# A fused attention and feed-forward layer: weight loads in halves, small pieces of side work, and last-stage buffers moved

## The chip, the cores and the metric

The kernel runs on one NeuronCore of a Trainium2 chip. The metric is device time in microseconds (us) of one execution. PE is TensorE, DVE is VectorE, ACT is ScalarE, POOL is GpSimd, and SP is the engine whose queue issues every DMA of this kernel.

## The reference

The input x has 4 batches of 512 rows and 1024 columns. Everything is float32. Attention has 32 heads of 32 columns, one shared key and value head, a linear bias and a causal mask. The second part is a linear layer whose weight comes from 6-bit codes.

```
def attn(h, Wq, Wkv, Wo):
    q = (h @ Wq).reshape(b, s, 32, 32)
    k, v = (h @ Wkv)[..., :32], (h @ Wkv)[..., 32:]
    scores = einsum('bqhd,bkd->bhqk', q, k) * 32 ** -0.5 + slopes * (pos_k - pos_q)
    attn = softmax(where(pos_k <= pos_q, scores, -inf))
    return einsum('bhqk,bkd->bqhd', attn, v).reshape(b, s, 1024) @ Wo

def ffn(x, qweight, scale, zero, bias):
    w = (unpack(qweight) - zero) * scale          # 1024 x 1024 codes of 6 bits
    return x @ w.T + bias

x = x + attn(layernorm(x), Wq, Wkv, Wo)
x = x + ffn(layernorm(x), qweight, scale, zero, bias)
```

## The kernel before

Each engine has a program written out by hand; an engine waits on semaphores, and what stands behind a waiting instruction waits too. Float32 factors are split into a high and a low part (`woh` and `wol`, `osh` and `osl`, `yth` and `ytl`), and products of the parts are summed.

There are three stages. The **first** normalises x, projects it, writes q to the tensors `qh_d` and `ql_d` in DRAM, and turns the codes into a weight `wi_d` in DRAM. The **second** is attention in 32 steps; step s is group s % 8 (four heads) of batch s // 8. The **third** goes over 16 tiles of 128 rows: `out_proj(t)` multiplies by Wo, `norm(t)` adds x and normalises, `turn_y(t)` transposes, `ffn(t)` multiplies by the codes `wi`, `result(t)` adds scale, shift and bias, and `store(t)` writes.

**A step of attention.** On PE a step has 12 places: places 0 to 4 and 6 to 11 hold a unit of transposed scores (`score_t`, L586), place 5 holds `turn_max(s+1)` (L576), the transpose of the maxima of the next step. Between them lie the 16 products of `score` (L559), 28 products ahead, and the products with the values (L597) and with ones (L610, `totals`) of step s-1. The maxima of the scores come from DVE (`maximum`, L920), 16 in a step; product n may start only when DVE has taken what was in its bank of PSUM, about one head earlier. After the tenth maximum (i = 9) DVE makes `ml`, the low part of the maxima of step s+1 (`max_low`, L927); the unit at place 8 on PE waits for `ml`, since it reuses that bank. SP then sends `mh` and `ml` (L302) into rows of q of step s+1, and place 0 of that step waits for them to land. q of step s lies in `qst[s % 4]`, a quarter of `xt0`; SP loads it three steps ahead (L294, 0.77 MB in three DMAs). ACT takes the exponentials (L761, `exponentials(s, k)`, k from 0 to 10), POOL cuts them by the mask (L415) and adds them up (L422, L428).

**Side work in the steps.** SP loads two chunks of `wi` (L333, 512 KB each) in each of the steps 1 to 4. In eight steps (WO_STEPS) Wo is split: SP loads a chunk of 512 KB into `ob`, ACT rounds it (`wo_high`, L777, after k = 9) and DVE subtracts (`wo_low`, L937, 128x1024, behind the sixteen maxima). In steps 10 to 13, 18 to 21 and 26 to 29 DVE inverts a quarter of the sums of a batch (`invert`, L933). In step 26 SP issues `load_o(0)`, `load_o(1)` (L351, 512 KB each) and `load_inv(0)` (L360, four DMAs of 128 KB).

**From the second stage to the third.** PE mixes out_proj(0) into the last step and behind it, then the totals of step 31, then `out_proj(1)`. ACT ends the steps with exponentials(31, 10), then take_o, take_sums, `o_high(1)` (L799). `o_high(1)` needs `o_normal(1)` on DVE (L955), and that needs load_inv(1). SP, behind the steps: load_inv(1), store_o(31), a wait for the totals of step 31, then x for tile 0 (`load_x2`, L344), three broadcast rows (L390), x for tile 1, load_o(2), load_inv(2). All buffers of the third stage but `osh0`, `osl0`, `ob` and `inv_b` lie where `pt`, the exponentials, lay. On ACT the order is std_y(0), o_high(2), t_high(0), so ffn(0) waits for load_inv(2) by way of `o_normal(2)` on POOL (L434).

## Time and profile before

| | us |
|---|---|
| median of 3 runs | 929.73 |
| lowest and highest | 925.4, 939.7 |
| profiled execution, whole | 931.09 |
| its span, first to last instruction | 929.3 |

The profiled execution is one of its own; 1.8 us of it lie outside the span. Rows below are read against it.

### The profile page before, as it was taken

How to read it: one execution, taken by the hardware profiler on the slowest of the kernel's cores; microseconds unless marked ns; L12 is line 12 of the kernel's file. 1: busy time of each engine (PE TensorE's matmuls, PEld its weight loads, DVE VectorE, ACT ScalarE, POOL GpSimd, SP SyncE). 2: the span in 40 equal slices, each digit the busy share in tenths (PEclk: the TensorE clock that was granted, in tenths of full speed). 3: DMA queues.
4: the chain of work that ended last, by engine and by line, in shares of the span. 5: the costliest groups of instructions: out<-in, count | busy, mean ns of one | idle time of the engine just before them, and what ended most of it. 6: DMA issues, size and time to landing. Idle time of an engine off the chain costs nothing.

```text
span 929.3 us, 13775 instructions
## 1 busy us (share of the span) xinstructions
PE 872.2 (94%) x4912; PEld 628.3 (68%) x4912; DVE 542.0 (58%) x1469; ACT 335.4 (36%) x639; POOL 397.0 (43%) x254
## 2 busy tenths in 40 slices
PE   2799999999999999999999979969999999999996
PEld 2578888888855555555555545548888888888884
DVE  6454362532566787888788757126656455554553
ACT  2422222221066666667666636321211112211110
POOL 0000000000048778888888858626345433454211
PEclk9899999999979999999999979988999999999997
DMA  4544554648348754464454461175333553334111
GB/s 153 164 156 122 176 153 153 176 120 212 101 107 225 201 140 106 115 165 117 111 145 130 114 143 46 48 202 139 90 91 93 145 124 105 90 91 135 47 46 45
DMA packets 86892, 117.17 MB, mean 126 GB/s; under 512 B 8020, under 2 KB 50004, under 8 KB 86744
## 3 DMA queue, kind: packets, MB, share of 16 engines
q1 hardware_dynamic: 86824, 116.30, 46.2%
q8 instruction: 39, 0.64, 0.3%
...
## 4 chain that ended last, share of the span: by engine, by line
PE 87%; DMA 5%; DVE 5%; ACT 1%; SPq 1%; issue 1%; POOL 0%; DVEq 0%; POOLq 0%; ACTq 0%
PE p_o L505 19%; PE p_st L668 14%; PE p_st L586 10%; PE p_s L654 10%; PE p_s L559 9%; PE p_o L597 9%; PE p_o L654 8%; PE p_o L610 4%; DMA xt<-ml 2%; PE p_st L505 2%; PE p_s L498 1%; DMA raw<-in_wq_dram 1%; DVE spill L920 1%; DMA inv_b<-inv_d 1%; PE p_st L576 1%
## 5 line engine op out<-in xcount | busy, mean ns | idle before, releaser
L920 DVE CUSTOM_DVE_ANT_0 spill<-p_s,mask 128x128 bf16<-128x128 f32 (+3 forms) x512 | 225.4, 486 | 82.3 <-PE p_s L559 80.6
L415 POOL TENSOR_SCALAR_AFFINE_SELECT pt<-pt 128x512 f32<-128x512 f32 x128 | 90.1, 716 | 317.2 <-ACT pt L761 317.2
L761 ACT ACTIVATE pt<-p_st 128x512 f32<-128x512 f32 (+1 forms) x352 | 181.4, 561 | 102.0 <-PE p_st L586 96.6
L505 PE MATMUL p_o<-xt,wqh 128*128 128x512 f32 x512 | 171.8, 402 | 3.7 <-DVE wql L1021 3.7
L559 PE MATMUL p_s<-kst,xt 98*128 98x128 f32 (+3 forms) x512 | 152.3, 336 | 6.5 <-DVE mx L920 6.5
L586 PE MATMUL p_st<-xt,kst 100*128 100x512 f32 (+1 forms) x352 | 148.5, 425 | 8.4 <-DMA xt<-ml 6.4
L505 PEld LDWEIGHTS p_o<-xt,wqh 128*128 128x128 f32 x512 | 98.3, 192 | 24.8 <-DVE wql L1021 4.1
L559 PEld LDWEIGHTS p_s<-kst,xt 98*128 98x128 f32 x512 | 101.0, 200 | 20.0 <-issue 9.7
L422 POOL TENSOR_TENSOR pt<-pt 128x1536 f32<-128x1536 f32 x32 | 111.7, 3490 | 2.7
L586 PEld LDWEIGHTS p_st<-xt,kst 100*128 100x128 f32 x352 | 68.3, 195 | 63.6 <-ACT pt L761 27.7
L505 PE MATMUL p_o<-xt,wql 128*128 128x512 f32 x256 | 101.5, 396 | 0.0
L438 POOL TENSOR_TENSOR osl<-ob,osh 128x1024 fp32r<-128x1024 f32 x14 | 33.6, 2400 | 136.6 <-ACT osh L799 136.5
L597 PE MATMUL p_o<-pt,vst 128*32 128x512 f32 (+3 forms) x1024 | 91.6, 452 | 0.0
L668 PE MATMUL p_st<-wi,yth 128*128 128x512 f32 x256 | 84.2, 411 | 6.5 <-DVE ytl L983 6.5
L668 PE MATMUL p_st<-wi,ytl 128*128 128x512 f32 x256 | 83.3, 407 | 0.0
L428 POOL TENSOR_TENSOR pt<-pt 128x1024 f32<-128x1024 f32 x32 | 76.3, 2385 | 0.0
L905 DVE TENSOR_TENSOR ql<-p_o,qh 128x512 fp32r<-128x512 f32 x32 | 22.1, 692 | 76.5 <-ACT qh L734 76.5
L734 ACT CAST qh<-p_o 128x512 fp32r<-128x512 f32 x32 | 18.8, 587 | 125.2 <-PE p_o L505 125.2
L445 POOL TENSOR_TENSOR xr<-xr,bias_b 128x1024 f32<-128x1024 f32 x16 | 50.6, 3161 | 30.8 <-ACT y L808 30.8
L668 PEld LDWEIGHTS p_st<-wi,yth 128*128 128x128 f32 x256 | 50.1, 197 | 19.2 <-issue 4.0
L814 ACT CAST yth<-p_s 128x512 fp32r<-128x512 f32 x16 | 9.4, 586 | 149.0 <-PE p_s L680 149.0
L668 PEld LDWEIGHTS p_st<-wi,ytl 128*128 128x128 f32 x256 | 50.2, 196 | 12.5
...
## 6 DMA issues: line engine op xcount, KB each, us to landing
...
```

What stands on the lines that cost most here:

```text
L415: pool.affine_select(out=own, in_=own, compare_op=ALU.is_ge, fill=0.0, base=0, pattern=[[0, 4], [1, P]], channel_multiplier=-1).then_inc(c ...
L422: pool.tensor_tensor(p[:, :, ADD_AT:ADD_AT + 3 * P], p[:, :, PT_AT[0] + P:PT_AT[0] + S], p[:, :, PT_AT[1]:PT_AT[1] + 3 * P], ALU.add).then ...
L428: pool.tensor_tensor(to, to, p[:, :, PT_AT[2]:PT_AT[2] + 2 * P], ALU.add).then_inc(add_done, 1)
L445: pool.tensor_tensor(xr[:, t % 2, :], xr[:, t % 2, :], bias_b[:, :], ALU.add).then_inc(res_bias, 1)
L505: last = pe.matmul(dst, w[:, c, cols], xs[:, c, :], start=(c == 0 and k == 0), stop=(c == CK - 1 and k == 2))
L559: pe.matmul(scores_of(n), qst[s % 4][0:R_MAX, j, qb * P:(qb + 1) * P], kst[0:R_MAX, b * S:b * S + keys], start=True, stop=True).then_inc(s ...
L586: pe.matmul(p_st[:, place(k) % 3, 0:heads * KB_LEN[kb]], kst[0:R_END, b * S + kb * P:b * S + (kb + 1) * P], qst[s % 4][0:R_END, j:j + head ...
L597: last = pe.matmul(p_o[32 * h:32 * h + 32, kb * P:S], vst[:, TPB * b + kb, :], pt[s % 2][:, h, PT_AT[kb]:PT_AT[kb] + KB_LEN[kb]], start=(k ...
L654: last = pe.matmul(p_wo[t % 2][:, n, :], a[:, c, :], w[:, c, n * S:(n + 1) * S], start=(c == 0 and k == 0), stop=(c == CK - 1 and k == 2))
L668: last = pe.matmul(p_ff[:, n, :], a[:, c, :], wi[:, c, n * S:(n + 1) * S], start=(c == 0 and a is yth), stop=(c == CK - 1 and a is ytl))
L761: act.activation(pt[s % 2][:, j:j + heads, PT_AT[kb]:PT_AT[kb] + KB_LEN[kb]], p_st[:, place(k) % 3, 0:heads * KB_LEN[kb]].rearrange("p (j ...
L920: dve.tensor_tensor_reduce(spill[:, SPILL_AT[qb]:SPILL_AT[qb] + keys], scores_of(n), mask[:, S - keys:S], 1.0, LOWEST, ALU.add, ALU.max, m ...
```

## The change

- Wo is loaded in 16 halves of a chunk (256 KB), one in each of the steps 1 to 16 (`load_wo`); ACT rounds half h in step h + 2, DVE subtracts it in step h + 3, in two pieces of 128x256, behind the maxima i = 3 and i = 11.
- The codes are loaded in 16 halves, one in each of the steps 17 to 31 and one behind them (`load_wi`).
- A reciprocal of 128 columns becomes four of 32, behind the maxima i = 1, 5, 9 (there behind `ml`) and 13.
- load_o(0) and load_o(1) come in quarters of 128 KB, one in each of the steps 21 to 28; load_inv(0) stays in step 26.
- `xt0` is given up after the second stage: `osh1`, `osl1`, `xr`, `yth0`, `ytl0`, `y` and `yth1` lie in it. `yth` and `ytl` become two buffers each. x for tiles 0 and 1 is loaded in step 31, ahead of load_inv(1). `o_high(1)` moves on ACT to between k = 9 and k = 10 of step 31. DVE no longer waits for the broadcast rows ahead of norm(0).
- `turn_y(t + 1)` goes one chunk of out_proj earlier; turn_y(15) goes into ffn(14), behind chunk 5. The last pieces of out_proj(0) stand in another order among the values of step 31.
- The last tile is done in halves of 512 columns: product, result and store.

VectorE, attention. `spill,mx<-p_s,mask` is one maximum (width by qb: 128, 256, 384, 512 keys), `mx` its result; before, the end of a step of WO_STEPS and the start of the next:

```order
L920 ISA spill,mx<-p_s,mask 128x384
L920 ISA mx 128x1
L920 ISA spill,mx<-p_s,mask 128x512
L920 ISA mx 128x1
L937 TENSOR_TENSOR wol<-ob,woh 128x1024
L920 ISA spill,mx<-p_s,mask 128x128
```

The same engine after the change, in the middle of step 3, from maximum i = 3 on:

```order
L947 ISA spill,mx<-p_s,mask 128x512
L947 ISA mx 128x1
L965 TENSOR_TENSOR wol<-ob,woh 128x256
L947 ISA spill,mx<-p_s,mask 128x128
L947 ISA mx 128x1
L947 ISA spill,mx<-p_s,mask 128x256
L947 ISA mx 128x1
L947 ISA spill,mx<-p_s,mask 128x384
L947 ISA mx 128x1
L947 ISA spill,mx<-p_s,mask 128x512
```

One block of 1024 columns behind a step has become two pieces of 256 inside each of sixteen steps; the first stands between the maxima i = 3 and i = 4, seven instructions ahead of the 512-key maximum i = 7, and `ml` follows two maxima later.

ScalarE, the end of step 31 (`pt1` holds its exponentials, `sums` the totals of batch 3), before:

```order
L761 ACTIVATE pt1<-p_st 128x2x256
L761 ACTIVATE pt1<-p_st 128x4x128
L768 COPY o_st<-p_o2 128x512
L773 COPY sums<-p_o2 128x512
L799 CAST osh1<-ob 128x1024
```

and after:

```order
L787 ACTIVATE pt1<-p_st 128x2x256
L825 CAST osh1<-ob 128x1024
L787 ACTIVATE pt1<-p_st 128x4x128
L794 COPY o_st<-p_o2 128x512
L799 COPY sums<-p_o2 128x512
```

The rounding of tile 1 now stands ahead of the last exponentials of the stage.

SP, from the last store of o but one on, before:

```order
L308 DMA o_d<-o_st 128x512
L360 DMA inv_b<-inv_d 32x8x128 x4
L308 DMA o_d<-o_st 128x512
L344 DMA xr<-in_x_dram 128x1024
L390 DMA scale_b<-in_w_scale_dram 128x1024
```

and after:

```order
L316 DMA o_d<-o_st 128x512
L324 DMA wi<-wi_d 128x512
L358 DMA xr<-in_x_dram 128x1024 x2
L375 DMA inv_b<-inv_d 32x8x128 x4
L324 DMA wi<-wi_d 128x512
L316 DMA o_d<-o_st 128x512
L411 DMA scale_b<-in_w_scale_dram 128x1024
```

Both loads of x and a half of `wi` now go ahead of the load of `inv_b`.

The core of the diff:

```diff
...
-WO_STEPS = (6, 7, 8, 14, 15, 16, 22, 23)
+HALVES = 2 * CK
...
-        xt0 = sb("xt0", [P, 2 * CK, S], F32R)
-        qst = [xt0[:, 4 * i:4 * i + 4, :] for i in range(4)]
...
         with ExitStack() as stage:
             sb = tensors(stage)
+            xt0 = sb("xt0", [P, 2 * CK, S], F32R)
+            qst = [xt0[:, 4 * i:4 * i + 4, :] for i in range(4)]
...
+        sb = tensors(ctx)
+        osh1, osl1 = sb("osh1", [P, CK, P], F32R), sb("osl1", [P, CK, P], F32R)
+        xr = sb("xr", [P, 2, D])
+        yth0, ytl0 = sb("yth0", [P, CK, P], F32R), sb("ytl0", [P, CK, P], F32R)
+        y, yth1 = sb("y", [P, D]), sb("yth1", [P, CK, P], F32R)
...
-            osh1, osl1 = sb("osh1", [P, CK, P], F32R), sb("osl1", [P, CK, P], F32R)
-            yth, ytl = sb("yth", [P, CK, P], F32R), sb("ytl", [P, CK, P], F32R)
-            xr = sb("xr", [P, 2, D])
-            y = sb("y", [P, D])
+            ytl1 = sb("ytl1", [P, CK, P], F32R)
             yo = sb("yo", [P, 2, D])
...
-            def load_wo(c):
-                at_least(sp, wo_lo, c - 1)
-                sp.dma_start(ob[:, c % 2, :], wo_v[:, c, :]).then_inc(wo_in[c % 2], 16)
+            def load_wo(h):
+                at_least(sp, wo_lo, 2 * (h - 3))
+                sp.dma_start(wo_half(ob, h), wo_v[:, h // 2, S * (h % 2):S * (h % 2) + S]).then_inc(wo_in[h % 4], 16)
...
+            def load_wi(h):
+                at = (slice(None), h // 2, slice(S * (h % 2), S * (h % 2) + S))
+                sp.dma_start(wi[at].bitcast(F32), wi_d[at]).then_inc(wi_in, 16)
...
-                if s in (1, 2, 3, 4):
-                    for c in (2 * s - 2, 2 * s - 1):
-                        sp.dma_start(wi[:, c, :].bitcast(F32), wi_d[:, c, :]).then_inc(wi_in, 16)
-                if s + 1 in WO_STEPS:
-                    load_wo(WO_STEPS.index(s + 1))
-                if s == STEPS - 6:
-                    load_o(0)
-                    load_o(1)
+                if 1 <= s <= HALVES:
+                    load_wo(s - 1)
+                if s > HALVES:
+                    load_wi(s - HALVES - 1)
+                if 21 <= s < 29:
+                    load_o((s - 21) // 4, (s - 21) % 4)
+                if s == 26:
                     load_inv(0)
+                if s == STEPS - 1:
+                    load_x2(0)
+                    load_x2(1)
...
-                    sp.wait_ge(wo_lo, CK)
+                    sp.wait_ge(wo_lo, 2 * HALVES)
...
+                of = slice(2 * part, 2 * part + 2)
+                sp.dma_start(ob[:, t % 2, :].rearrange("p (g q) -> p g q", g=GROUPS)[:, of, :],
+                             o_v[:, of, t * P:(t + 1) * P]).then_inc(o_in[t % 2], 16)
...
+                if t < TILES - 1:
+                    sp.wait_ge(out_done, t + 1)
+                    sp.dma_start(out_rows[t * P:(t + 1) * P, :], yo[:, t % 2, :]).then_inc(stored[t % 2], 16)
+                else:
+                    for n in range(2):
+                        half = slice(n * S, n * S + S)
+                        sp.wait_ge(out_done, t + 1 + n)
+                        sp.dma_start(out_rows[t * P:(t + 1) * P, half], yo[:, t % 2, half]).then_inc(stored[t % 2], 16)
...
             load_inv(1)
+            load_wi(HALVES - 1)
             store_o(STEPS - 1)
             sp.wait_ge(pv_done, STEPS)
-            load_x2(0)
...
-            load_x2(1)
-            load_o(2)
-            load_inv(2)
-            load_o(3)
-            load_inv(3)
+            for t in (2, 3):
+                for part in range(4):
+                    load_o(t, part)
+                load_inv(t)
...
-                for c in range(CK):
-                    for a in (yth, ytl):
-                        for n in range(2):
-                            last = pe.matmul(p_ff[:, n, :], a[:, c, :], wi[:, c, n * S:(n + 1) * S],
-                                             start=(c == 0 and a is yth), stop=(c == CK - 1 and a is ytl))
-                last.then_inc(ff_done, 1)
+                for halves in ((0, 1),) if t < TILES - 1 else ((0,), (1,)):
+                    for c in range(CK):
+                        for low, a in enumerate((yth[t % 2], ytl[t % 2])):
+                            for n in halves:
+                                last = pe.matmul(p_ff[:, n, :], a[:, c, :], wi[:, c, n * S:(n + 1) * S],
+                                                 start=(c == 0 and low == 0), stop=(c == CK - 1 and low == 1))
+                        if t == TILES - 2 and c == 5:
+                            turn_y(t + 1)
+                    last.then_inc(ff_done, 1)
...
-            for kb in range(4):
-                values(STEPS - 1, kb)
-                out_proj(0, 4 + kb)
+            values(STEPS - 1, 0)
+            out_proj(0, 4)
+            values(STEPS - 1, 1)
+            out_proj(0, 5)
+            values(STEPS - 1, 2)
+            values(STEPS - 1, 3)
+            out_proj(0, 6)
             for part in range(2):
                 totals(STEPS - 1, part)
+            out_proj(0, 7)
...
                     ffn(t)
                 if t + 2 < TILES:
-                    for c in range(6):
-                        out_proj(t + 2, c)
-                if t + 1 < TILES:
-                    turn_y(t + 1)
-                if t + 2 < TILES:
-                    for c in range(6, CK):
+                    for c in range(CK):
+                        if c == 5:
+                            turn_y(t + 1)
                         out_proj(t + 2, c)
...
-                    if k == 9 and s in WO_STEPS:
-                        wo_high(WO_STEPS.index(s))
+                    if k == 9 and 0 <= s - 2 < HALVES:
+                        wo_high(s - 2)
                     if k == 9 and s == STEPS - 2:
                         o_high(0)
+                    if k == 9 and s == STEPS - 1:
+                        o_high(1)
...
                 act.wait_ge(o_norm, t + 1)
                 at_least(act, wo_done, t - 1)
-                if t == 1:
-                    act.wait_ge(pv_done, STEPS)
                 act.copy(flat(osh[t % 2][:, :, :]), ob[:, t % 2, :]).then_inc(o_hi, 1)
...
             def t_high(t):
-                at_least(act, ff_done, t)
+                at_least(act, ff_done, t - 1)
+                if t == 1:
+                    act.wait_ge(pv_done, STEPS)
...
-            o_high(1)
             std_y(0)
             o_high(2)
...
-                of = slice(part * P, (part + 1) * P)
+                of = slice(part * 32, part * 32 + 32)
...
+            def wo_low(h, part):
+                dve.wait_ge(wo_hi, h + 1)
+                of = slice(256 * part, 256 * part + 256)
+                dve.tensor_tensor(wo_half(wol, h)[:, of], wo_half(ob, h)[:, of], wo_half(woh, h)[:, of],
+                                  ALU.subtract).then_inc(wo_lo, 1)
...
                         maximum(first + i)
                     if i == 9 and s + 1 < STEPS:
                         max_low(s + 1)
-                if s > GROUPS and s % GROUPS in (2, 3, 4, 5):
-                    invert(s // GROUPS - 1, s % GROUPS - 2)
-                if s in WO_STEPS:
-                    wo_low(WO_STEPS.index(s))
+                    if i % 4 == 1 and s > GROUPS and s % GROUPS in (2, 3, 4, 5):
+                        invert(s // GROUPS - 1, 4 * (s % GROUPS - 2) + i // 4)
+                    if i in (3, 11) and 0 <= s - 3 < HALVES:
+                        wo_low(s - 3, i // 8)
...
+                        dve.wait_ge(ff_done, t + 1 + n)
+                        dve.tensor_tensor(to[:, half], p_ff[:, n, :], scale_b[:, half], ALU.mult).then_inc(scaled, 1)
+                        dve.wait_ge(scaled, t + 1 + n)
+                        dve.wait_ge(res_done, t + 1)
+                        dve.tensor_tensor(to[:, half], to[:, half], xs[:, half], ALU.add).then_inc(out_done, 1)
...
             o_low(1)
-            dve.wait_ge(rows_in, 48)
             norm(0)
...
                 if t < 4:
-                    invert(LASTB, t)
+                    for part in range(4):
+                        invert(LASTB, 4 * t + part)
```

## Rows read from the trace of the kernel before

**Rows 1.** Windows: PE, PEld, DVE, ACT, POOL busy (instructions), clock, DMA, GB/s.
```profile
627.00:913.00 286.00, 283.30 (x1272) 230.67 (x1271) 158.11 (x169) 51.42 (x88) 115.11 (x43) 0.99 0.37 98
```

**Rows 2.** Waits of the whole span: engine, line, waited for; us in total, times, longest.
```profile
PEld p_st L586 <- DMA xt<-ml: 9.4, 6, 5.2
...
PE p_s L559 <- DVE mx L920: 6.5, 8, 0.8
...
PE p_st L586 <- DMA xt<-ml: 6.4, 3, 4.7
```

**Rows 3.** Timeline of PE, place 5 of four steps: start, us, instruction.
```profile
323.87 0.33 PE L576 MATMUL p_st<-ident,mx 128*128 128x128 f32 x1
...
334.67 0.33 PE L576 MATMUL p_st<-ident,mx 128*128 128x128 f32 x1
...
447.34 0.33 PE L576 MATMUL p_st<-ident,mx 128*128 128x128 f32 x1
...
457.08 0.33 PE L576 MATMUL p_st<-ident,mx 128*128 128x128 f32 x1
```

**Rows 4.** Timeline of DVE, behind step 6 and inside step 18.
```profile
330.48 1.95 DVE L937 TENSOR_TENSOR wol<-ob,woh 128x1024 fp32r<-128x1024 f32 x1
...
448.05 0.69 DVE L920 CUSTOM_DVE_ANT_0 spill<-p_s,mask 128x512 bf16<-128x512 f32 x1 [0.37 <-PE p_s L559]
...
449.22 0.27 DVE L927 SCALAR_TENSOR_TENSOR ml<-p_st,mh 16x128 fp32r<-16x128 f32 x1
...
452.66 0.56 DVE L920 CUSTOM_DVE_ANT_0 spill<-p_s,mask 128x384 bf16<-128x384 f32 x1 [1.03 <-PE p_s L559]
```

**Rows 5.** Timeline of PE's weight loads, place 8 of that step.
```profile
449.55 0.19 PEld L586 LDWEIGHTS p_st<-xt,kst 100*128 100x128 f32 x1 [0.23 <-DVE ml L927]
```

**Rows 6.** Groups by form: count, busy us, mean ns, idle before.
```profile
L937 DVE TENSOR_TENSOR wol<-ob,woh 128x1024 fp32r<-128x1024 f32 x8 | 15.6, 1946 | 0.7
L933 DVE RECIPROCAL sums<-sums 128x128 f32<-128x128 f32 x16 | 15.1, 947 | 0.0
...
L977 DVE RECIPROCAL mv<-mv 128x1 f32<-128x1 f32 x16 | 2.5, 157 | 0.0
```

**Rows 7.** Windows around the long wait for `ml` of step 28; columns as in Rows 1.
```profile
531.50:547.60 16.10, 11.37 (x92) 6.41 (x84) 10.03 (x41) 7.43 (x16) 14.41 (x10) 0.99 0.98 209
...
547.60:557.00 9.40, 9.39 (x33) 4.85 (x33) 3.57 (x15) 3.42 (x7) 1.17 (x2) 0.50 0.19 41
```

**Rows 8.** Timeline of ACT, last exponentials and `o_high(1)`.
```profile
593.17 0.60 ACT L761 ACTIVATE pt<-p_st 128x512 f32<-128x512 f32 x1 [1.02 <-PE p_st L586]
...
603.99 1.05 ACT L799 CAST osh<-ob 128x1024 fp32r<-128x1024 f32 x1
```

**Rows 9.** Timeline of DVE, `o_normal(1)`.
```profile
597.02 1.23 DVE L955 TENSOR_TENSOR ob<-ob,inv_b 128x1024 f32<-128x1024 f32 x1 [13.40 <-DMA inv_b<-inv_d]
```

**Rows 10.** Timeline of POOL, last sum of step 31 and `o_normal(2)`.
```profile
594.44 2.38 POOL L428 TENSOR_TENSOR pt<-pt 128x1024 f32<-128x1024 f32 x1
621.14 2.37 POOL L434 TENSOR_TENSOR ob<-ob,inv_b 128x1024 f32<-128x1024 f32 x1 [24.32 <-DMA inv_b<-inv_d]
```

**Rows 11.** Timeline of PE, totals of step 31 and start of `out_proj(1)`.
```profile
602.15 1.28 PE L610 MATMUL p_o<-pt,pick 128*32 128x512 f32 x16
606.35 0.73 PE L654 MATMUL p_o<-woh,osh 128*128 128x512 f32 x2 [2.91 <-DVE osl L959]
```

**Rows 12.** Windows: the loads of x and rows, columns as in Rows 1.
```profile
605.00:614.00 9.00, 7.65 (x33) 6.19 (x34) 2.69 (x3) 1.32 (x2) 0.00 (x0) 1.00 1.01 331
```

**Rows 13.** Timeline of PE, `turn_y(15)` and start of `ffn(15)`.
```profile
909.26 0.60 PE L680 MATMUL p_s<-ident,y 128*128 128x128 f32 x4
...
913.20 1.22 PE L668 MATMUL p_st<-wi,yth 128*128 128x512 f32 x2 [2.90 <-DVE ytl L983]
```

**Rows 14.** Timeline of DVE, the end: `t_low(15)` and `result(15)`.
```profile
911.87 0.68 DVE L983 TENSOR_TENSOR ytl<-p_s,yth 128x512 fp32r<-128x512 f32 x1
...
923.70 1.23 DVE L994 TENSOR_TENSOR yo<-p_st,scale_b 128x1024 f32<-128x1024 f32 x1 [9.37 <-PE p_st L668]
```

More of the change, by code:

```diff
@@ L150, in layer @@
         osh, osl = (osh0, osh1), (osl0, osl1)
+        yth, ytl = (yth0, yth1), (ytl0, ytl1)
         p_s = ctx.enter_context(nc.psum_tensor("p_s", [P, 3, S], F32))
@@ L189, in layer @@
         o_out, inv_out = sem("o_out"), sem("inv_out")
-        wo_in = [sem(f"wo_in{i}") for i in range(2)]
+        wo_in = [sem(f"wo_in{i}") for i in range(4)]
         wo_hi, wo_lo, wi_in = sem("wo_hi"), sem("wo_lo"), sem("wi_in")
@@ L405, in _ @@
                     load_x2(t + 2)
-            for i in range(2):
-                sp.wait_ge(stored[i], 16 * (TILES // 2))
+            sp.wait_ge(stored[0], 16 * (TILES // 2))
+            sp.wait_ge(stored[1], 16 * (TILES // 2) + 16)
         @block.gpsimd
@@ L810, in t_high @@
             def t_high(t):
-                at_least(act, ff_done, t)
+                at_least(act, ff_done, t - 1)
+                if t == 1:
+                    act.wait_ge(pv_done, STEPS)
                 for half in range(2):
                     act.wait_ge(turned, 2 * t + half + 1)
-                    act.copy(yth[:, 4 * half:4 * half + 4, :], p_tr3[half]).then_inc(t_hi, 1)
+                    act.copy(yth[t % 2][:, 4 * half:4 * half + 4, :], p_tr3[half]).then_inc(t_hi, 1)
             act.wait_ge(consts, 5)
@@ L982, in t_low @@
                     part = slice(4 * half, 4 * half + 4)
-                    dve.tensor_tensor(ytl[:, part, :], p_tr3[half], yth[:, part, :], ALU.subtract).then_inc(t_lo, 1)
+                    dve.tensor_tensor(ytl[t % 2][:, part, :], p_tr3[half], yth[t % 2][:, part, :], ALU.subtract).then_inc(t_lo, 1)
             def result(t):
@@ L991, in result @@
                                          op0=ALU.mult, op1=ALU.add).then_inc(res_done, 1)
[L992 removed]
                 at_least(dve, stored[t % 2], 16 * (t // 2))
[L994 to L997 removed]
+                if t < TILES - 1:
+                    dve.wait_ge(ff_done, t + 1)
+                    dve.tensor_tensor(to, flat(p_ff), scale_b[:, :], ALU.mult).then_inc(scaled, 1)
+                    dve.wait_ge(scaled, t + 1)
+                    dve.wait_ge(res_done, t + 1)
+                    dve.tensor_tensor(to, to, xs, ALU.add).then_inc(out_done, 1)
+                else:
+                    for n in range(2):
+                        half = slice(n * S, n * S + S)
+                        dve.wait_ge(ff_done, t + 1 + n)
+                        dve.tensor_tensor(to[:, half], p_ff[:, n, :], scale_b[:, half], ALU.mult).then_inc(scaled, 1)
+                        dve.wait_ge(scaled, t + 1 + n)
+                        dve.wait_ge(res_done, t + 1)
+                        dve.tensor_tensor(to[:, half], to[:, half], xs[:, half], ALU.add).then_inc(out_done, 1)
             dve.memset(mv[:, :, :], 0.0).then_inc(q_freed, 2)
@@ L1040, in _ @@
                 if t < 4:
-                    invert(LASTB, t)
+                    for part in range(4):
+                        invert(LASTB, 4 * t + part)
 def build(nc, x, wq, wkv, wo, qweight, w_scale, w_zero, bias, kpos, slopes, out):
```

36 lines of the change are left out of this document (13 added, 23 removed).

## The prediction

> **What bounds the kernel now.** I read the windows by stage first, then the waits, then the timelines of the places that they name.
>
> In the third stage PE is busy for 283.3 of 286.0 us at the full clock [rows 1]. There the way to the end is PE's own work; what the change moves between ffn and out_proj (turn_y one chunk earlier, two buffers of `yth`) has nothing to win, since no wait is left.
>
> The waits show where PE stands still in attention [rows 2]. Eight waits on DVE's maxima cost 6.5 us; they stand in the eight steps of WO_STEPS, one in each. Three waits for `ml` to land (a DMA) cost 6.4, one of them 4.7. The marks at place 5 give what a step takes [rows 3]: 334.67 - 323.87 = 10.80 with a subtraction of Wo behind the maxima, 457.08 - 447.34 = 9.74 in a step that has an `invert` behind them. So a block of 1.95 us on DVE [rows 4, 6] costs PE 1.06, and one of 0.95 nothing.
>
> **Part 1, blocks of `wo_low` gone: 8 x 1.06 = 8.5 us** less [rows 3] (the seven others look the same).
>
> **Part 2, the pieces put in their place.** A piece is a quarter of 1946 ns. Its price lies between 0.49 (a quarter) and (1946 - 157) / 4 + 157 = 0.60 us, if 157 ns, the time of a one-column instruction, is the fixed part [rows 6]. A reciprocal of 32 columns costs (947 - 157) / 4 + 157 = 0.36. DVE's gaps in a plain step decide what of it shows [rows 4]: 0.37 us ahead of i = 7, and 1.03 ahead of i = 14. The second piece (behind i = 11) falls into the 1.03 and is free. The first (behind i = 3) has only the 0.37 before `ml`, and `ml` is tight: the weight load at place 8 waits for it already, 0.23 us [rows 5], so a later `ml` holds PE one to one. That makes 0.12 to 0.23 in each of the 11 steps that have only pieces. In the five steps that also invert (10 to 13 and 18) the reciprocal behind i = 5 comes on top: 0.48 to 0.59. Sum: 11 x 0.12 + 5 x 0.48 = 3.7, to 11 x 0.23 + 5 x 0.59 = 5.5. I take 4.5, in the middle, since POOL adds beside the first piece much as beside the block that these prices come from. The lower bound is 0, if PE has slack that the 0.23 hides. Net of parts 1 and 2: -4.0 (range -8.5 to -3.0). ACT rounds 16 halves in place of 8 chunks; its block of a whole chunk held nobody (the eight waits name DVE), so half of one doesn't.
>
> The Trainium skill says in VectorE: DVE Perf Modes, section on the trn2 errata, that a Vector instruction whose source is SBUF pays a fixed latency once, and that many small tiles pay it per tile, so tiles should have at least 512 columns. The 157 ns above is of that size. This rule speaks against the pieces of 256 and 32 columns; what it would make of the sum is rival 4.
>
> **Part 3, loads of `wi` no longer 1 MB a step.** Of the waits for `ml` two on PE (6.4 - 4.7 = 1.7 us) and five on the weight loads (9.4 - 5.2 = 4.2) are the short ones [rows 2]; the ones on PE follow the steps with two loads of `wi`. Now a step has 256 KB of side loads, 384 in steps 21 to 28. I take 2.2 off (1.7 to 4.2), nearer to PE's own waits, as a weight load's wait is partly covered. Steps with a 512 KB chunk of Wo show no wait for `ml`, so 256 to 384 KB should show none.
>
> **Part 4, step 26.** Here 1 MB of `ob`, 0.5 MB of `inv_b` and q of step 30 stand in the queue ahead of `ml` of step 28. The DMA engines are at 0.98 for 16.1 us with 209 GB/s [rows 7]; PE waits 4.7 us, and then its clock is at 0.50, which is 1.2 GHz, for 9.4 us. Half of that is lost again: 4.7 + 4.7 = 9.4 us. Now the step has 256 KB of `wi`, 128 of `ob` and the same 0.5 MB of `inv_b`: 0.64 MB less, which at 209 GB/s is 3.1 us less. That leaves up to 4.7 - 3.1 = 1.6 us of wait, 0 if `inv_b` overlaps better; I take 0.8, and no loss of clock, since the two short waits cost none. Part 4: -8.6 (range -9.4 to -7.0; if the clock still falls, rival 2).
>
> **Part 5, the end of step 31, where the change adds a wait.** o_high(1) on ACT now stands ahead of exponentials(31, 10). It waits for o_normal(1), that for load_inv(1), and behind it are queued the exponentials, the last cut and the last sum on POOL, values and totals on PE. Ahead of load_inv(1) SP now issues 0.25 MB of `wi` and 1 MB of x. Before, `inv_b` was there at 597.02 [rows 9]. At 331 GB/s, what the same kinds of loads reach [rows 12], 1.25 MB are 3.8 us: 600.8. Then o_normal 1.2 [rows 9] and o_high 1.05 [rows 8]: the exponentials start at 603.1 instead of 593.17 [rows 8], 9.9 later. POOL's last sum ends at 594.44 + 2.38 + 9.9 = 606.7 [rows 10]. PE has values(31, 3), a chunk of out_proj(0) and the totals left, after a hole of some 5 us; after 4.7 us it had the half clock [rows 7], so the totals (1.28 [rows 11]) take some 1.9 and end at 608.6. Before they ended at 606.35 - 2.91 = 603.4 [rows 11]. So the release of SP behind them comes 5.2 later. Against that the 1 MB of x is gone from the queue behind it, 3.2 us at 331 GB/s, so `inv_b` of tile 2, which POOL had at 621.14 [rows 10], comes 5.2 - 3.2 = 2.0 us later, and ffn(0) hangs on it over POOL and ACT. That norm(0) no longer waits for the rows gives nothing, as its tile waits for this anyway. Part 5: +2.0. If the transfers of x don't delay `inv_b`, the totals end at 606.7 - 3.8 + 1.3 = 604.2, and the part is +0.8 - 3.2 = -2.4; if they go at the 209 GB/s of rows 7, 2.2 us more, +4.2.
>
> **Part 6, the last tile.** turn_y(15) moves from behind ffn(14) into it: the products of ffn(14) end 910.30 - 909.26 = 1.0 us later (913.20 - 2.90 is the end of the turn) [rows 13]. It was hidden before, since ffn(15) waits for t_low(15), and that stands on DVE behind result(14), which waits for ffn(14) [rows 14]; that order stays. So +1.0. result(15) on the way to the end is two instructions of 1.23; in halves of 0.68, as long as a subtraction of 512 columns [rows 14], it is -1.1, and the store is 256 KB shorter, 0.8 us at 331 GB/s. Part 6: -0.9 (range -2 to 0). The clock at ffn(15) is low with a hole of 2.9 us; with 3.9 it will be too.
>
> **Sum:** -8.5 + 4.5 - 2.2 - 8.6 + 2.0 - 0.9 = -13.7 us. The profiled execution took 931.1, so 917.4 by its measure; the median of the three runs is 929.7, 1.4 lower. I say **917**. Its own range is 911 to 924.
>
> **Rivals.**
> 1. **It gives more: 908.** All pieces are covered (part 2 at 1.0), step 26 is clean (-9.4), part 5 ends at -2.4: -8.5 + 1.0 - 2.2 - 9.4 - 2.4 - 0.9 = -22.4, or 908.7 by the profile and 907.3 by the median. For it speak DVE's gaps, 1.4 us in a step by rows 4 alone; against it the weight load that waits for `ml` now. Chance 0.25.
> 2. **Step 26 isn't cured: 924.** The 0.5 MB of `inv_b` in short rows stays in that step. A wait of 2.9 us was followed by a pair of products of 1.22 us in one place and of 0.73 in another [rows 11, 13], so near that length the clock may fall or not. If it falls after a wait of 3, PE pays 3 and some 3.8 more: part 4 is -2.6 instead of -8.6, and the sum -7.7, with the worse end of part 5 -6. Chance 0.15.
> 3. **Slower: the queue paces every step: 936.** Side loads now stand in 31 steps, ahead of q and so of `ml`. If a step's 1.3 to 1.4 MB took longer than 9.74 us, each step would wait; 0.6 us in 31 steps are 18.6, less the 13.7 gives +5 or more. It decides at 1.4 MB / 9.74 us = 144 GB/s. Against it: 209 GB/s in the full window [rows 7]. Chance 0.04.
> 4. **No gain: the pieces pay for themselves: 929.** DVE has 24 more subtractions and 36 more reciprocals in the steps, at 157 ns each 9.4 us. If those came on top of the old 8.5, because DVE's total and not the place of the block sets the step, the sum is -13.7 + 4.0 + 9.4 = -0.3, near 931 by the profile. Against it: 0.95 us of reciprocal behind a step costs nothing [rows 3]. The rule of the Trainium skill that stands in part 2 is this mechanism. Chance 0.04.
>
> The forecast keeps 0.52. Below 2% (18.6 us, about what a measurement of this kernel can tell from no change) the line is 911.1: rival 1 lies under it, with a little of the forecast's own range, so faster 0.27; slower by 2% is only the far part of rival 3, 0.02; the rest is 0.71. The range 906 to 926 takes in rivals 1 and 2.
>
> **What the profile after should show.** Part 1: no waits of 0.8 on `mx`; steps 6 to 8 below 10.2. Part 2: longer waits for `ml` at place 8 in steps 3 to 18, most in 10 to 13. Part 4: a wait for `ml` of step 28 under 1.6 us and a full clock behind it. Part 5: a hole on PE of about 5 us ahead of values(31, 3), ACT waiting for o_normal(1), ffn(0) not nearer to the end of the last step than before. Part 6: halves at the end. I am wrong if POOL's port makes the pieces far longer than 0.6, if the clock falls where I have it full, or if x and `inv_b` don't queue as I say.

## The result and the profile after

The changed kernel takes **956.11 us** (median of 5 runs, 954.51 to 960.0) against 929.73 (5 runs, 925.4 to 939.7; three of them are those of the table before): ratio 1.0286, interval 1.0238 to 1.0334. It is 26.4 us slower. The prediction, 917 with a range of 906 to 926, is wrong. Its profiled execution took 960.0 us (span 958.3) at a mean clock of 0.955.

The windows by stage, after the change (start and end, length, then busy us of PE, PEld, DVE, ACT, POOL with the instructions in brackets, the granted clock, the DMA share, GB/s):

```profile
284.00:493.00 209.00, 190.70 (x1305) 107.94 (x1301) 163.10 (x624) 117.70 (x243) 145.65 (x103) 0.89 0.47 113
493.00:590.00 97.00, 96.27 (x752) 55.22 (x755) 76.65 (x350) 63.32 (x130) 81.13 (x61) 1.00 0.61 154
...
600.00:659.00 59.00, 42.89 (x251) 25.98 (x252) 13.15 (x14) 17.50 (x32) 26.30 (x17) 0.88 0.48 119
659.00:940.00 281.00, 281.00 (x1268) 229.16 (x1267) 152.01 (x177) 51.40 (x88) 114.84 (x43) 0.99 0.37 99
```

The same first stretch of the kernel before:

```profile
284.00:493.00 209.00, 202.35 (x1568) 115.02 (x1560) 165.96 (x692) 137.77 (x275) 174.71 (x123) 1.00 0.56 143
```

Two places stand out. In steps 3 to 18 PE stands still for 18.3 us instead of 6.7 and loses clock, 0.89 for 209 us; this stretch holds some 17 steps now and held some 20 before. The rest of attention, with step 26, is clean. Between the stages (600 to 659) PE stands still for 16 us. The third stage is full, as in [rows 1].

The waits after the change, to be read against [rows 2]:

```profile
PEld p_s L580 <- DVE mx L947: 22.5, 15, 2.4
...
PE p_s L580 <- DVE mx L947: 17.6, 11, 2.1
...
PE p_st L690 <- DVE ytl L1012: 10.9, 2, 7.0
...
PE p_o L618 <- POOL pt L436: 8.4, 1, 8.4
...
PE p_st L607 <- DMA xt<-ml: 2.7, 2, 1.9
...
PE p_st L607 <- DVE ml L954: 1.6, 4, 0.9
```

PE's waits for `ml` to land fell from 6.4 to 2.7 us, of which 1.94 lies ahead of step 3 (at 266.50); those for maxima rose from 6.5 to 17.6. Marks of `turn_max` in steps 3, 4 and 5, with the wait and the totals between them (PE):

```profile
294.40 0.33 PE L597 MATMUL p_st<-ident,mx 128*128 128x128 f32 x1
...
305.87 0.33 PE L597 MATMUL p_st<-ident,mx 128*128 128x128 f32 x1
...
308.67 0.49 PE L580 MATMUL p_s<-kst,xt 98*128 98x128 f32 x2 [2.07 <-DVE mx L947]
...
312.41 2.36 PE L631 MATMUL p_o<-pt,pick 128*32 128x512 f32 x16
...
321.01 0.33 PE L597 MATMUL p_st<-ident,mx 128*128 128x128 f32 x1
```

From the first mark to the second are 11.47 us, and from there to the third 321.01 - 305.87 = 15.14, the longest interval of all, against 9.74 in [rows 3]. Of the 5.4 more, 2.07 are the wait. The totals take 2.36 us instead of 1.28 [rows 11]: the clock behind the wait is at half, 1.2 GHz:

```profile
310.50:317.00 6.50, 6.50 (x28) 4.00 (x28) 2.84 (x12) 3.38 (x7) 4.87 (x3) 0.50 0.31 84
```

6.5 us at half speed do 3.25 us of work; 2.07 + 3.25 = 5.3, so the step is accounted for. What DVE did then, and POOL beside it (two timelines; the price that the prediction gave the piece was 0.49 to 0.60 us):

```profile
304.48 0.69 DVE L947 CUSTOM_DVE_ANT_0 spill<-p_s,mask 128x512 bf16<-128x512 f32 x1 [0.79 <-PE p_s L580]
305.09 0.08 DVE L947 DVE_READ_ACCUMULATOR2_ANT mx<- 128x1 f32 x1
305.09 2.97 DVE L965 TENSOR_TENSOR wol<-ob,woh 128x256 fp32r<-128x256 f32 x1
307.98 0.28 DVE L947 CUSTOM_DVE_ANT_0 spill<-p_s,mask 128x128 bf16<-128x128 f32 x1
```

```profile
304.82 2.38 POOL L449 TENSOR_TENSOR pt<-pt 128x1024 f32<-128x1024 f32 x1
307.15 0.64 POOL L436 TENSOR_SCALAR_AFFINE_SELECT pt<-pt 128x512 f32<-128x512 f32 x1
```

The piece of Wo takes 2.97 us, five to six times that price. It starts 0.27 us behind the start of POOL's addition and ends at 308.06, 0.27 us behind the end of POOL's next instruction (307.79). The 32 pieces, in the groups by form:

```profile
L965 DVE TENSOR_TENSOR wol<-ob,woh 128x256 fp32r<-128x256 f32 x32 | 37.7, 1180 | 0.0
```

They run from 0.42 to 2.97 us, mean 1.18. I compared each with POOL: of the 16 first pieces (behind i = 3) eleven start in the earlier part of L449, with 1.5 us or more of it left, and last 1.8 to 3.0; the five that start in its last 0.4 us or behind it take 0.42 to 0.68; the second pieces (behind i = 11) meet a short L436 and take 0.42 or 0.51. The maxima, one operand of which is in PSUM, keep their times beside POOL.

Between the stages, the rows that answer to [rows 8 to 11] (ACT; DVE; POOL; PE):

```profile
628.94 1.04 ACT L825 CAST osh<-ob 128x1024 fp32r<-128x1024 f32 x1 [12.10 <-DVE ob L984]
629.89 0.59 ACT L787 ACTIVATE pt<-p_st 128x512 f32<-128x512 f32 x1
```

```profile
627.68 1.23 DVE L984 TENSOR_TENSOR ob<-ob,inv_b 128x1024 f32<-128x1024 f32 x1 [19.35 <-DMA inv_b<-inv_d]
```

```profile
631.70 2.35 POOL L449 TENSOR_TENSOR pt<-pt 128x1024 f32<-128x1024 f32 x1
```

```profile
631.78 0.66 PE L618 MATMUL p_o<-pt,vst 128*32 128x128 f32 x8 [8.42 <-POOL pt L436]
...
635.23 2.36 PE L631 MATMUL p_o<-pt,pick 128*32 128x512 f32 x16
...
658.48 1.19 PE L690 MATMUL p_st<-wi,yth 128*128 128x512 f32 x2 [7.01 <-DVE ytl L1012]
```

ACT stands for 12.1 us at `o_high(1)` with the last exponentials behind it, PE then for 8.4, and the totals run at half clock.

**Where the 29 us of the profiled executions went.** By the marks on PE: up to step 3 +1.9; steps 3 to 18 +33.1; the rest of attention -10.3 (of it -8.2 around step 26); from the last mark to ffn(0) 58.6 instead of 51.4, +7.2; from there to the end -3.0. Sum +28.9, and 960.0 - 931.1 = 28.9. Steps 3 to 18 by marks (294.40 to 492.13):

```profile
294.40:492.13 197.73, 179.43 (x1220) 101.58 (x1217) 154.16 (x586) 110.09 (x225) 135.81 (x97) 0.88 0.46 111
```

Here 17.6 us are waits for maxima, and a clock of 0.88 over 197.7 us is some 24 us of full-speed work lost (an estimate from the row). The clock costs more than the waits themselves.

### The profile page after: what moved, and what is told of

It reads as the page before. It is cut to its first block, busy times and chain, and to the rows that moved or that the text cites. A ratio compares the mean times of both kernels' runs of the same rounds, so it can differ in the third digit from the quotient of the medians.

```text
span 958.3 us, 13970 instructions
## 1 busy us (share of the span) xinstructions
PE 887.2 (93%) x4912; PEld 636.3 (66%) x4912; DVE 559.6 (58%) x1543; ACT 334.9 (35%) x647; POOL 393.6 (41%) x254
## 4 chain that ended last, share of the span: by engine, by line
PE 85%; DVE 5%; issue 3%; DMA 3%; ACT 2%; POOL 1%; SPq 1%; DVEq 0%; POOLq 0%; ACTq 0%
PE p_o L526 18%; PE p_st L690 13%; PE p_st L607 10%; PE p_s L580 9%; PE p_s L675 9%; PE p_o L675 8%; PE p_o L618 8%; PE p_o L631 4%; PE p_st L526 2%; DVE spill L947 1%; PE p_s L519 1%; DMA raw<-in_wq_dram 1%; DMA inv_b<-inv_d 1%; PE p_st L597 1%; DMA xt<-ml 1%
## 5 line engine op out<-in xcount | busy, mean ns | idle before, releaser
L436 POOL TENSOR_SCALAR_AFFINE_SELECT pt<-pt 128x512 f32<-128x512 f32 x128 | 84.8, 673 | 358.0 <-ACT pt L787 357.5
L580 PE MATMUL p_s<-kst,xt 98*128 98x128 f32 (+3 forms) x512 | 157.6, 347 | 17.6 <-DVE mx L947 17.6
L607 PE MATMUL p_st<-xt,kst 100*128 100x512 f32 (+1 forms) x352 | 154.0, 440 | 5.7 <-DMA xt<-ml 2.7
L580 PEld LDWEIGHTS p_s<-kst,xt 98*128 98x128 f32 x512 | 105.3, 208 | 33.7 <-DVE mx L947 22.5
L607 PEld LDWEIGHTS p_st<-xt,kst 100*128 100x128 f32 x352 | 72.2, 206 | 60.0 <-ACT pt L787 28.7
L618 PE MATMUL p_o<-pt,vst 128*32 128x512 f32 (+3 forms) x1024 | 94.0, 464 | 8.4 <-POOL pt L436 8.4
L449 POOL TENSOR_TENSOR pt<-pt 128x1024 f32<-128x1024 f32 x32 | 76.2, 2383 | 0.0
L760 ACT CAST qh<-p_o 128x512 fp32r<-128x512 f32 x32 | 18.8, 587 | 125.2 <-PE p_o L526 125.2
L690 PEld LDWEIGHTS p_st<-wi,ytl 128*128 128x128 f32 x256 | 49.3, 193 | 12.1
L526 PEld LDWEIGHTS p_o<-xt,wql 128*128 128x128 f32 x256 | 49.1, 192 | 8.9
```

The costliest lines, as they stand in the source:

```text
L436: pool.affine_select(out=own, in_=own, compare_op=ALU.is_ge, fill=0.0, base=0, pattern=[[0, 4], [1, P]], channel_multiplier=-1).then_inc(c ...
L449: pool.tensor_tensor(to, to, p[:, :, PT_AT[2]:PT_AT[2] + 2 * P], ALU.add).then_inc(add_done, 1)
L526: last = pe.matmul(dst, w[:, c, cols], xs[:, c, :], start=(c == 0 and k == 0), stop=(c == CK - 1 and k == 2))
L580: pe.matmul(scores_of(n), qst[s % 4][0:R_MAX, j, qb * P:(qb + 1) * P], kst[0:R_MAX, b * S:b * S + keys], start=True, stop=True).then_inc(s ...
L607: pe.matmul(p_st[:, place(k) % 3, 0:heads * KB_LEN[kb]], kst[0:R_END, b * S + kb * P:b * S + (kb + 1) * P], qst[s % 4][0:R_END, j:j + head ...
L618: last = pe.matmul(p_o[32 * h:32 * h + 32, kb * P:S], vst[:, TPB * b + kb, :], pt[s % 2][:, h, PT_AT[kb]:PT_AT[kb] + KB_LEN[kb]], start=(k ...
```

## Experiments

Each ratio is against the kernel before, measured beside it on the same chip (930.8 to 931.0 us there). The first four ask why the pieces are long.

**Both pieces behind i = 11.**

```diff
-                    if i in (3, 11) and 0 <= s - 3 < HALVES:
-                        wo_low(s - 3, i // 8)
+                    if i == 11 and 0 <= s - 3 < HALVES:
+                        wo_low(s - 3, 0)
+                        wo_low(s - 3, 1)
```

> The changed kernel, with both pieces of a half of Wo behind maximum i = 11, none behind i = 3. Nothing else is altered. Theory P (place): a subtraction with both operands in SBUF that starts while POOL is in an addition waits for POOL's instruction to end; behind i = 3 it meets the last sum of a step, behind i = 11 it doesn't. Then all 32 pieces take 0.42 to 0.52 us, the holes of 1.4 to 2.1 us on PE in steps 3 to 18 go, and these 16 steps, 33 us longer than before the change, take 9.8 to 10.1 us each: 922 to 928 us in all. Rival N (number): many small instructions cost DVE their fixed part wherever they stand; then the time stays within 5 us of 956.

Measured: 1003.53 us, ratio 1.0791 (1.0735 to 1.0847), outside both sides of the expectation. The saving I expected fails, since the second piece now begins where POOL's longest addition begins. DVE (the row holds both pieces) and POOL:

```profile
294.58 4.11 DVE L965 TENSOR_TENSOR wol<-ob,woh 128x256 fp32r<-128x256 f32 x2
```

```profile
294.90 3.50 POOL L443 TENSOR_TENSOR pt<-pt 128x1536 f32<-128x1536 f32 x1
```

The pair ends at 298.69, 0.29 behind POOL's end, and the steps last 14.5 to 15.8 us. The number of pieces and their width are those of the changed kernel; only the place differs, and it costs 47 us more. That speaks against the number of pieces as the cause.

**The first piece with an operand in PSUM.** It stands ahead of maximum i = 4, which is where it stood. It reads scores in place of Wo, so this kernel leaves out the low part of half of Wo.

```diff
+                if i == 4 and 0 <= at - 3 < HALVES:
+                    dve.tensor_tensor(wo_half(wol, h)[:, 0:256], p_s[:, 0, 0:256], wo_half(woh, h)[:, 0:256],
+                                      ALU.subtract).then_inc(wo_lo, 1)
```

> The changed kernel, with the first piece at its place (between the maxima i = 3 and i = 4), but its first operand is 256 columns of scores in PSUM in place of Wo in SBUF. This leaves out the low part of half of Wo. Theory P, in the form that both operands in SBUF are needed for the wait on POOL: the piece takes 0.4 to 0.5 us beside POOL's addition, and the time falls to 922 to 930. If any subtraction that writes or reads SBUF waits for POOL, or if the place itself (between i = 3 and ml) is what costs, the pieces stay at up to 3 us, or the time above 945.

Measured: 917.34, ratio 0.9859 (0.9818 to 0.99), below the 922 to 930 expected. Groups by form:

```profile
L971 DVE TENSOR_TENSOR wol<-ob,woh 128x256 fp32r<-128x256 f32 x16 | 8.1, 508 | 0.0
L950 DVE TENSOR_TENSOR wol<-p_s,woh 128x256 fp32r<-128x256 f32 x16 | 6.7, 419 | 0.0
```

The same subtraction at the same place takes 0.42 us if one operand comes from PSUM, with 1.9 to 2.1 us of POOL's L449 still to run in each of the 16 steps, and the steps take 9.71 to 9.94. So neither DVE's total nor the count of instructions makes the steps long: it is the piece with both operands in SBUF beside POOL. The second pieces (L971, both in SBUF) still wait 0.1 us each for the end of a short L436.

**The reciprocals in blocks of 128 columns again.** `invert` behind the maxima, as before the change.

> The changed kernel, with the reciprocals in blocks of 128 columns behind the maxima of a step again. Theory P: the reciprocal has one SBUF input and isn't held by POOL; steps 10 to 13 and 18 lose 0.3 us each at most, so 951 to 956. Rival R (the reciprocals in small pieces are what delays ml): the steps 10 to 13 and 18 fall by 2 us and more, 946 or less.

Measured: 955.81, ratio 1.0273 (1.0224 to 1.0323), the changed kernel's time, as theory P had it. The small reciprocals cost nothing that shows.

**The same work at the right place: one subtraction of 512 columns directly behind `ml`.**

```diff
                     if i == 9 and s + 1 < STEPS:
                         max_low(s + 1)
-                    if i in (3, 11) and 0 <= s - 3 < HALVES:
-                        wo_low(s - 3, i // 8)
+                    if i == 9 and 0 <= s - 3 < HALVES:
+                        wo_low(s - 3)
```

> The changed kernel, but both pieces of a half are one subtraction of 512 columns, directly behind the subtraction that makes ml (behind i = 9), where GpSimd has nothing to do for about a microsecond. Theory A (a subtraction with both operands in SBUF that starts while GpSimd runs a tensor_tensor waits for its end, and only that makes steps 3 to 18 long): it starts beside an idle GpSimd, costs 0.68 us and lies in the gap ahead of i = 14; each step 9.73 to 9.85 us, total 917 to 924. Rival B (DVE's work in a step is too much, wherever it stands): the steps stay above 10.5, total over 935. Rival C (steps 3 to 18 are long from another part of the change, such as loads in every step): 950 or more.

Measured: **916.04**, ratio 0.9852 (0.9805 to 0.99), just under the 917 to 924 expected. DVE and POOL in a step:

```profile
304.33 0.27 DVE L954 SCALAR_TENSOR_TENSOR ml<-p_st,mh 16x128 fp32r<-16x128 f32 x1
304.53 0.67 DVE L964 TENSOR_TENSOR wol<-ob,woh 128x512 fp32r<-128x512 f32 x1
```

```profile
303.65 0.64 POOL L436 TENSOR_SCALAR_AFFINE_SELECT pt<-pt 128x512 f32<-128x512 f32 x1
305.70 0.64 POOL L436 TENSOR_SCALAR_AFFINE_SELECT pt<-pt 128x512 f32<-128x512 f32 x1 [1.41 <-ACT pt L787]
```

The subtraction of twice the width takes 0.67 us in the 1.4 us in which POOL waits for exponentials. No step from 3 on takes more than 10.04 us but the one with the wait for `ml` behind step 26 (10.74); PE is busy for 208.86 of the 209 us. Theory A holds, rivals B and C fall. The place of the pieces cost some 956.1 - 916.0 = 40 us; that there is one subtraction instead of two makes no difference to it, as the kernel with the PSUM operand has two and takes 917.34.

**`o_high(1)` behind take_sums again,** in the changed kernel.

```diff
-                    if k == 9 and s == STEPS - 1:
-                        o_high(1)
...
             take_sums(B - 1)
+            o_high(1)
```

> The changed kernel, with o_high(1) on ACT behind take_sums again; x is still loaded ahead of inv_b. Theory A (ACT's queue): the hole of 8.4 us on PE ahead of values(31, 3) goes, out_proj(0) and the totals end as before the change, and out_proj(1) waits for inv_b instead; the rows are released 9 us earlier, ffn(0) comes 6 to 9 us earlier: 947 to 951. Rival Q (the DMA queue alone): inv_b of tile 1 lands as late as now, and ffn(0) hangs on that; the time stays at 954 to 957.

Measured: 940.61, ratio 1.0115 (1.0071 to 1.0159), 15.5 us less than the changed kernel and more than I expected; rival Q falls. PE:

```profile
619.30 1.28 PE L631 MATMUL p_o<-pt,pick 128*32 128x512 f32 x16
624.90 0.73 PE L675 MATMUL p_o<-woh,osh 128*128 128x512 f32 x2 [2.71 <-DVE osl L987]
639.71 0.70 PE L690 MATMUL p_st<-wi,yth 128*128 128x512 f32 x2 [0.90 <-DVE ytl L1011]
```

The hole ahead of the last values is gone, and so is the one of 7.0 us ahead of ffn(0). From the last mark to ffn(0) are 45.7 us: 12.9 less than after the change, and 5.7 less than before it. The rest lies in the long steps: by the profiled executions (960.0 and 940.5) 12.9 of 19.5 us lie here and 5.8 ahead of the last mark, where the code is the same. Why the long steps vary so was not looked into.

**Both edits.**

> As the kernel with the one subtraction behind ml, and o_high(1) behind take_sums again. If the two causes are separate (theory): 15 us less than that kernel, 903 to 909. If o_high(1) ahead of the last exponentials costs its 15 us only because ACT and GpSimd ran late in the long steps: 915 to 922.

Measured: **903.81**, ratio 0.9729 (0.9689 to 0.9769), inside the expectation of the separate causes: 12.2 us less than with the first edit alone. This version beats both kernels.

**x behind inv_b in SP's queue,** with both edits: load_x2(0) and load_x2(1) leave step 31 and stand behind `store_o(31)`.

> As the kernel with both edits, and SP issues load_inv(1), the last 256 KB of wi and the store of the last step ahead of the 1 MB of x. Theory (x and inv_b go one after the other, at 209 to 331 GB/s): inv_b(1) lands 3 us earlier; since o_high(1) no longer holds the exponentials, the end of the step does not move, and the third stage starts 0 to 2 us earlier; total 0 to 2 us below the kernel with both edits. Rival (x doesn't delay inv_b): no difference in the landing either.

Measured: 906.31, ratio 0.9751 (0.9711 to 0.9791): 2.5 us above the kernel with both edits by medians, where I expected 0 to 2 below; the intervals overlap. DVE, `o_normal(1)` of that kernel, and then of the one with x behind:

```profile
585.43 1.23 DVE L981 TENSOR_TENSOR ob<-ob,inv_b 128x1024 f32<-128x1024 f32 x1 [19.34 <-DMA inv_b<-inv_d]
```

```profile
578.52 1.22 DVE L980 TENSOR_TENSOR ob<-ob,inv_b 128x1024 f32<-128x1024 f32 x1 [14.43 <-DMA inv_b<-inv_d]
```

Counted from the issue of the store of o in that step (573.47 and 571.48), `inv_b` of tile 1 lands after 12.0 and after 7.0 us. So the 1 MB of x delays it by 5 us, not 3. The start of ffn(0), in the same order:

```profile
604.12 0.70 PE L690 MATMUL p_st<-wi,yth 128*128 128x512 f32 x2 [1.16 <-DVE ytl L1009]
```

```profile
604.22 1.19 PE L689 MATMUL p_st<-wi,yth 128*128 128x512 f32 x2 [6.78 <-DVE ytl L1008]
```

From the last mark (557.63 and 555.76) to ffn(0) are 46.5 and 48.5 us, so the earlier `inv_b` of tile 1 brings nothing, and the stretch gets 2.0 longer. The x now stands ahead of `inv_b` of tile 2, which POOL has 25.2 us behind that store in the first kernel and 27.4 in the second, and ffn(0) hangs on it.

**o of tiles 0 and 1 whole in step 26,** with both edits.

```diff
-                if 21 <= s < 29:
-                    load_o((s - 21) // 4, (s - 21) % 4)
                 if s == 26:
+                    for t in range(2):
+                        for part in range(4):
+                            load_o(t, part)
```

> As the kernel with both edits, but the 1 MB of o for tiles 0 and 1 is loaded in step 26 as before the change, in eight loads of 128 KB. Theory (part 4 of the prediction: the 4.7 us wait for ml of step 28 and the half clock behind it come from that 1 MB): 7 to 9.4 us more than the kernel with both edits, a wait on ml of over 3 us in step 28. Rival (the 0.5 MB of inv_b in short rows makes that wait): under 2 us more.

Measured: 912.19, ratio 0.9829 (0.9776 to 0.9883), 8.4 us above the kernel with both edits. PE at step 28, with the clock behind it (windows):

```profile
539.64 0.80 PE L608 MATMUL p_st<-xt,kst 100*128 100x512 f32 x1 [5.32 <-DMA xt<-ml]
```

```profile
530.00:539.50 9.50, 4.32 (x39) 2.37 (x31) 4.35 (x21) 3.12 (x6) 8.02 (x6) 0.83 1.00 214
539.50:545.00 5.50, 5.36 (x24) 2.72 (x28) 2.18 (x12) 2.39 (x5) 0.11 (x2) 0.68 0.59 113
```

The wait of [rows 2] is back, with the DMA engines full at 214 GB/s, and the step takes 16.85 us instead of 11.03. The rival, `inv_b` alone, falls: with 128 KB of o in that step, it leaves 1.04 us of wait in the kernel with both edits.

**Are small pieces needed at all?** In the kernel before, the block of 1024 columns moved behind `ml`.

```diff
                     if i == 9 and s + 1 < STEPS:
                         max_low(s + 1)
+                    if i == 9 and s in WO_STEPS:
+                        wo_low(WO_STEPS.index(s))
```

> The kernel before the change with one edit: each of the eight blocks of wo_low, a subtraction of 1024 columns, stands directly behind ml (behind i = 9) of its step and not behind the last maximum. Theory (what it costs depends on where it stands against GpSimd's instructions): it starts while GpSimd is idle and takes 1.22 us instead of 1.95; the gap ahead of i = 14 is 1.03, so at most 0.2 us shows on PE instead of 1.06, and the kernel is 6.9 to 8.5 us faster than before. Rival (the saving needs the small pieces): the steps of WO_STEPS keep 0.8 us or more of wait on the maxima, gain under 2 us.

Measured: 978.5, ratio 1.0522 (1.0478 to 1.0566): 48 us slower. Both sides of the expectation missed a wait. DVE, then POOL:

```profile
337.91 1.89 DVE L937 TENSOR_TENSOR wol<-ob,woh 128x1024 fp32r<-128x1024 f32 x1 [4.45 <-ACT woh L777]
```

```profile
335.28 3.44 POOL L422 TENSOR_TENSOR pt<-pt 128x1536 f32<-128x1536 f32 x1
```

ACT rounds the chunk only behind k = 9 of the same step, so DVE stands 4.45 us with the maxima queued behind it, and PE 4.02 us in each of the eight steps, with the clock lost behind it (16.6 to 16.9 us a step). The block also falls beside POOL's addition. With the block one step later (`if i == 9 and s - 1 in WO_STEPS`):

> The kernel before the change with one edit, mended: each of the eight blocks of wo_low stands directly behind ml (behind i = 9) of the step after its own, so that ACT has rounded the chunk long before. Theory (place against GpSimd and against ACT's rounding is all that counts, not the size): the block starts beside an idle GpSimd and takes 1.22 us, no step of WO_STEPS or behind it is over 10.0, 6.9 to 8.5 us faster than before: 920 to 924. Rival (the saving needs small pieces): 0.5 us or more of wait in each of the eight steps, gain under 4 us.

Measured: 924.34, ratio 0.9924 (0.9894 to 0.9954), 6.7 us faster by the medians: just under the saving that I expected, and above the rival's 4 (the interval is 4.3 to 9.9 us).

```profile
336.48 1.20 DVE L937 TENSOR_TENSOR wol<-ob,woh 128x1024 fp32r<-128x1024 f32 x1
```

The block takes 1.20 us instead of 1.95 [rows 4], and the steps that hold it 9.73 to 10.01 instead of 10.80 [rows 3]. That one move gives most of what part 1 was worth. What the change had beside the small size, and I didn't look at, is the whole step between ACT's rounding and DVE's subtraction.

**The last tile whole,** with both edits: product, result and store of tile 15 in one.

> The kernel with both edits, but the last tile's products, its result and its store are whole again, as before the change; turn_y(15) stays inside ffn(14). By part 6 of the prediction: 1.9 us more than the kernel with both edits (1.1 of result, 0.8 of the store), as the 1.0 of turn_y stays in both. If the halves' second products cost a wait of their own: 0 to 1.

Measured: 906.72, ratio 0.9751 (0.9724 to 0.9778), 2.9 us above the kernel with both edits by medians of separate runs. In the traces, from the start of result(14) to the end of result(15): 885.38 to 899.86 in halves, 884.23 to 900.83 whole, 14.5 against 16.6 us. Part 6 of the prediction put the halves at 1.9.

**`t_high(0)` ahead of `o_high(2)` on ACT,** with both edits.

> The kernel with both edits, and t_high(0) ahead of o_high(2) on ACT. Theory (part 5 of the prediction: ffn(0) hangs on inv_b of tile 2 over GpSimd's o_normal(2) and ACT's o_high(2), which stands ahead of t_high(0)): ffn(0) starts about 8 us earlier, out_proj(2) then waits for the low part of tile 2 until some 607, and 3 to 5 us are left: 899 to 901. Rival (the start of the third stage is held by something else, such as y of tile 0): no difference.

Measured: 902.97, ratio 0.9693 (0.9659 to 0.9728), 0.8 us below the kernel with both edits, which was measured on another chip: not told apart. The low part of y is ready at 600.02 instead of 603.97, but ffn(0) starts at 602.56, since until then PE is at work on out_proj(1). I had the wait right and its cover wrong: 1.16 us was all that stood open.

## Why the prediction was wrong

**Part 1** (-8.5) held, if a little high: the block moved to a free place is worth 6.7 alone by medians, with an interval of 4 to 10.

**Part 2 is the step that failed.** I put a piece at 0.49 to 0.60 us by dividing the block's 1946 ns by four, and wrote that POOL adds beside the first piece "much as beside the block that these prices come from". But the 1.95 was no price of the work. POOL before the change, beside the block of [rows 4] at 330.48:

```profile
327.84 3.50 POOL L422 TENSOR_TENSOR pt<-pt 128x1536 f32<-128x1536 f32 x1
```

It ends at 331.34: 0.86 us of the block is waiting for it, and the rest, 1.09, is the work (1.20 where POOL is idle). The work shrinks with the width: 1.20 us for 1024 columns, 0.67 for 512, 0.42 for 256. A wait doesn't; it depends on what POOL still has to run when the piece comes. Behind the sixteenth maximum that was 0.9 us, behind the fourth it is up to 2.7, two of POOL's instructions in a row. The Trainium skill says this in SBUF — State Buffer, section "SBUF: two separate sides": the port pair that VectorE and GpSimd share is an exclusive lock, a VectorE instruction with two SBUF inputs needs it against a GpSimd instruction that reads SBUF, and whoever starts second is blocked for the whole of the other's instruction. The trace agrees: the long pieces end 0.27 to 0.29 us behind POOL's end, and with a PSUM operand they take 0.42 us. In five of the eleven long pieces POOL's next instruction went first as well, as at 307.15. I named POOL's port as a way to be wrong and gave it no price and no chance; the range and its rival on the other side (rival 3, at 936) were therefore too low. The second half of the error is the clock, which the part did not price: of PE's eleven waits in these steps, 0.86 to 2.07 us long, nine were followed by half clock. And the waits fell on the products of `score`, which wait for the maxima, while I only priced `ml` being late by 0.12 to 0.59; PE's waits for `ml` from DVE are 1.6 us in the whole span.

In size: steps 3 to 18 are 33.1 us longer, though six of the eight blocks (6 x 1.06 = 6.4) and the 2.2 of part 3 are gone from them, so the pieces cost 33.1 + 6.4 + 2.2 = 41.7 us, not 4.5. The waits and the clock (17.6 + 24) and the kernel with the moved subtraction (40 less) say the same.

**Part 3** (-2.2) held: the two steps of 10.95 and 10.69 us before are 9.71 to 9.74 with the pieces in a free place, together 2.2.

**Part 4** (-8.6) held: step 28's interval went from 18.26 to 10.72, -7.5, with 0.73 of wait where I had 0.8 and the clock at 1.00 behind it, and undoing it alone costs 8.4.

**Part 5** (+2.0, range -2.4 to +4.2) had the mechanism and missed the size: +7.2. `inv_b` of tile 1 came 12.0 us behind the store's issue instead of 6.0, so +6.0 where I had +3.8: x costs 5 us in the queue, not 3.2. The hole was 8.4 us, not 5. From the start of the last exponentials to the end of the totals it took 637.59 - 629.89 = 7.7 us where I had 5.5: I let the totals start at the end of POOL's last sum (634.05) and put the values and the chunk of out_proj(0) ahead of them, which I named, at nothing. They took 3.45 us at half clock, and PE came to the totals at 635.23; the totals took 2.36 us, not 1.9. Behind the totals the stretch to ffn(0) became 2.2 us shorter, where I had 3.2. Without the move of `o_high(1)` the part would have been -5.7. Of that the early x brings 2.0 (46.5 against 48.5 us in the two kernels of that experiment), and the rest was not taken apart; the early `o_high(1)` is a loss of 11 to 13 (12.9 in the changed kernel; 57.6 - 46.5 between the two kernels with the moved subtraction).

**Part 6** (-0.9, range -2 to 0) held in sign; measured -3.0 from ffn(0) to the end, and -1.1 in the kernel with the subtraction behind `ml`, whose last stage is the same; so this stretch varies by some 2 us by itself. The hole ahead of ffn(15) is 3.84 us against 2.90 in [rows 13], +0.9 where I had +1.0; the halves give 2.1 by the traces, where I had 1.9.

**The rivals.** 1 falls with parts 2 and 5, and 2 with part 4 (no loss of clock). 3 falls: no wait for `ml` to land in the common step. 4 suspected the right thing: the pieces cost more than they bring, but not by a fixed part each, as the kernels with 16 and with 32 subtractions (916.0 and 917.3), none of which waits long, show no difference. So a fixed cost of each small piece does not explain the loss.

That the kernel with the moved subtraction took 916.0, next to my 917, is partly luck. By its own trace against the one before: up to step 3 +0.2, the steps behind it -18.8, where parts 1 to 4 sum to -14.8 (part 2 costs next to nothing there, not +4.5); to ffn(0) +6.2 instead of +2.0; to the end -1.1 instead of -0.9. That is -13.4 by the unrounded marks, and two errors of some 4 us cancel.
